# Gathers of a feed-forward layer's results add into X in place, two batches by turns

## The reference, cut to what matters

```python
x = x + tanh(g_xattn[0]) * L0_xattn(layernorm(x), ctx, ...)      # 16 heads
x = x + tanh(g_ffn[0])   * L0_ffn(layernorm(x), ...)             # 32 experts, top 4, and a shared one
x = x + tanh(g_xattn[1]) * L1_xattn(layernorm(x), ctx, ctx)      # 8 heads
x = x + tanh(g_ffn[1])   * L1_ffn(layernorm(x), ...)             # 8 experts, top 2, and shared ones

# the end of L0_ffn: each token sums four rows of the experts' results
gathered = ye[e_flat, minimum(pos, CAP - 1)]
gathered = where(valid, gathered, 0.0) * topk_w
routed   = gathered.reshape(T, K, D).sum(axis=1)
return routed + relu2(h @ shared_up_w.T) @ shared_down_w.T
```

## Time and profile before

| | us |
|---|---|
| median of 3 runs | 777.53 (777.05 to 778.8) |
| the profiled execution's own time | 779.62 |
| its span | 777.4 |
| busy PE, DVE, ACT, POOL | 667.8, 531.6, 379.0, 324.1 |
| the 64 gathers on POOL (L268) | 68.9, from 375.2 to 504.7 |
| mean granted TensorE clock | 0.955 of full speed |

### The profile page before, as it was taken

How to read it: one execution, slowest core, us unless ns; L and a number is a source line. 1 busy time by engine, 2 the same in 40 slices (tenths; PEclk the granted TensorE clock), 3 DMA queues, 4 the chain that set the end, 5 groups by cost and what they waited for, 6 DMA issues and landing times.

```text
span 777.4 us, 13620 instructions
## 1 busy us (share of the span) xinstructions
PE 667.8 (86%) x4737; PEld 349.5 (45%) x4738; DVE 531.6 (68%) x1252; ACT 379.0 (49%) x630; POOL 324.1 (42%) x337
## 2 busy tenths in 40 slices
PE   3889999999999899688735788999977999888996
PEld 1233333333333367576402244444433476555763
DVE  3889888888895699155278899997736743222336
ACT  2057888878787344244314566676502213333320
POOL 3535353535011101753568878831100057666530
PEclk9999999999999999889956999999979999999999
DMA  6834343444311800446447778896530022222137
GB/s 164 176 92 122 97 113 96 135 140 130 106 33 38 265 13 2 121 138 184 125 116 190 185 185 205 209 217 158 140 110 28 1 57 83 72 75 66 56 97 258
DMA packets 106362, 93.23 MB, mean 120 GB/s; under 512 B 25205, under 2 KB 92954, under 8 KB 106104
## 3 DMA queue, kind: packets, MB, share of 16 engines
q1 hardware_dynamic: 93600, 67.67, 32.5%
q0 software_dynamic: 8352, 18.74, 8.9%
q10 hardware_dynamic: 4344, 5.97, 2.9%
HBM read 50.63 MB, written 16.01 MB: 86 GB/s over the span
## 4 chain that ended last, share of the span: by engine, by line
PE 56%; DVE 13%; issue 11%; POOL 9%; DMA 4%; ACT 2%; SPq 2%; another core or an unknown queue 1%; ACTq 0%; POOLq 0%; DVEq 0%
PE O L447 9%; PE S L404 9%; PE ST L1547 6%; POOL spare L268 6%; DVE mx L566 4%; PE ST L1473 2%; PE S L1564 2%; PE M L1564 2%; PE ST L943 2%; POOL QKc L279 2%; PE ST L412 2%; PE M L496 2%; DMA QS<-mxT 2%; SPq L165 2%; PE M L489 1%
## 5 line engine op out<-in xcount | busy, mean ns | idle before, releaser
L566 DVE TENSOR_REDUCE mx<-S 128x2 f32<-128x512 f32 x384 | 250.7, 684 | 35.8 <-PE S L404 33.9
L319 ACT ACTIVATE PX<-ST 128x1024 f32<-128x1024 f32 x192 | 195.8, 1022 | 88.2 <-PE ST L412 79.2
L404 PE MATMUL S<-QS 62*128 62x256 bf16 (+1 forms) x768 | 151.2, 292 | 41.6 <-DVE mx L566 28.4
L412 PE MATMUL ST<-QS 64*128 64x256 bf16 (+1 forms) x768 | 141.0, 278 | 7.3 <-DMA QS<-mxT 7.3
L447 PE MATMUL O<-PX,VA 128*32 128x256 f32 x1536 | 123.3, 394 | 0.1
L404 PEld LDWEIGHTS S<-QS 62*128 62x128 bf16 (+1 forms) x768 | 48.7, 97 | 158.2 <-DVE mx L566 95.7
L268 POOL DMA_INDIRECT spare<-ye,GI x64 | 68.9, 1077 | 30.4 <-DMA ye<-QKc 16.1
L1658 POOL DMA_INDIRECT PX<-xn,TI x39 | 39.9, 1022 | 63.4 <-DVE K1n L1847 39.7
L412 PEld LDWEIGHTS ST<-QS 64*128 64x128 bf16 (+1 forms) x768 | 53.4, 96 | 23.3 <-DMA QS<-mxT 9.8
L1547 PE MATMUL ST<-EGU,Cb 128*128 x156 | 54.2, 471 | 6.3 <-ACT Cb L1615 4.9
L786 POOL DMA_INDIRECT PX<-xn,TI x32 | 33.5, 1046 | 61.2 <-DVE spare L1183 44.1
(11 more groups left out here) (302 smaller groups left out, 1114.2 us busy)
## 6 DMA issues: line engine op xcount, KB each, us to landing
QS<-QKs SPq DMA_DIRECT2D x177, 128.0 KB
EGU<-in_ew SPq DMA_DIRECT2D x16, 256.0 KB, 2.8
xn<-spare SPq DMA_DIRECT2D x8, 512.0 KB, 5.7
ye<-QKc SPq DMA_DIRECT2D x32, 128.0 KB
VA<-in_val SPq DMA_DIRECT2D x16, 256.0 KB
spare<-yt SPq DMA_DIRECT2D x16, 256.0 KB, 6.3
Cb<-in_ctx SPq DMA_DIRECT2D x31, 128.0 KB
on<-OS SPq DMA_DIRECT2D x27, 128.0 KB
```

The lines of the kernel that those rows point to most:

```text
L319: e.activation(M["PX"][pair % 4][:, :], M["ST"][pair % 2][:, :], ACT.Exp, scale=A.scale).then_inc(A.exp, 1)
L404: got = e.matmul(M["S"][n % 2][:, 256 * a:256 * a + 256], QS[:, 0, 128 * a:128 * a + 128], QS[:, 1, :], start=True, stop=True)
L412: got = e.matmul(M["ST"][(NP * t + k // 2) % 2][:, 512 * u + 256 * a:512 * u + 256 * a + 256], QS[:, 1, 128 * a:128 * a + 128], QS[:, 0, : ...
L566: e.tensor_reduce(M["mx"][b % 2][:, :, A.row_of_max(head)], M["S"][n % 2][:, :].rearrange("p (a s) -> p a s", a=2), AX.X, ALU.max, negate= ...
```

## The change

From batch 2 on, a gather no longer writes a buffer: it adds its rows into X[b] in place, through the transfer's own adding (`compute_op=ALU.add`). Two such gathers of one batch must not be under way together, since each reads X and writes it back. So a gather waits until the previous one of its batch has landed, and the order of the gathers takes two batches by turns: (2,0), (3,0), (2,1), (3,1), and so on, as batch and choice. It also waits for the shared expert's addition of its group. The bounds check of the indirect transfer is not given for these gathers. VectorE sums only batches 0 and 1; for the others `statistics` waits for the four gathers. The counts by the ends of steps -4, -3 and -2 become 12, 18 and 20.

```diff
--- before.py
+++ after.py
@@ -106,6 +106,8 @@
 
         self.s0 = 0 if self.first else 2
 
+        self.summed = 2
+
         self.lead = H + 12 if self.first else H + 6
 
     def steps(self):
@@ -116,7 +118,7 @@
 
     def gathered(self, t):
 
-        return {-5: 8, -4: 10, -3: 14, -2: 18, -1: 24, 0: 30, 1: 36}.get(t, max(0, min(K0 * (t + (7 if t < 0 else 8)), K0 * NB)))
+        return {-5: 8, -4: 12, -3: 18, -2: 20, -1: 24, 0: 30, 1: 36}.get(t, max(0, min(K0 * (t + (7 if t < 0 else 8)), K0 * NB)))
 
     def late(self, b):
 
@@ -235,7 +237,7 @@
             loads(e, w, t)
 
 
-def attention_pool(e, w, A, M, meanwhile=lambda t: None):
+def attention_pool(e, w, A, M, meanwhile=lambda t: None, shared=None):
     H = A.H
 
     for t in A.steps():
@@ -264,6 +266,17 @@
 
         def gather(n):
             b7, k = n // K0, n % K0
+            if b7 >= A.summed:
+
+                b7, k = b7 - b7 % 2 + k % 2, K0 // 2 * (b7 % 2) + k // 2
+                w.wait_ge(shared, b7 // GB + 1)
+
+                w.wait_ge(A.ga[b7 % 3], A.ga0 + 16 * (K0 * (b7 // 3) + k))
+                e.indirect_dma_start(
+                    out=M["X"][:, b7, :], out_offset=None, in_=M["ye_d"],
+                    in_offset=bass.IndirectOffsetOnAxis(ap=M["GI"][:, b7, k:k + 1], axis=0),
+                    compute_op=ALU.add).then_inc(A.ga[b7 % 3], 16)
+                return
             w.wait_ge(A.ca, 3 * (b7 - 2))
             e.indirect_dma_start(
                 out=M["GA"][b7 % 3][:, T * k:T * k + T], out_offset=None, in_=M["ye_d"],
@@ -547,8 +560,10 @@
         if b >= 2 * U:
 
             w.wait_ge(M["w_g"], 32)
-        if not A.first:
+        if not A.first and b < A.summed:
             w.wait_ge(A.ca, 3 * (b + 1))
+        elif not A.first:
+            w.wait_ge(A.ga[b % 3], A.ga0 + 16 * K0 * (b // 3 + 1))
         e.bn_stats(M["st6"][b % 2][:, :], M["X"][:, b, :]).then_inc(A.stat, 1)
         w.wait_ge(A.stat, 2 * b + 1)
         w.wait_ge(A.xn, b - 1)
@@ -656,12 +671,7 @@
                                     M["rs"][b0 % 2][:, 0:1], ALU.subtract, ALU.mult).then_inc(A.xn, 1)
                 if k in (3, 4) and within(b0) and b0 < A.helped:
                     parts(b0, k - 3)
-                if t == -2 and k == 4 or t == -1 and k == 0:
-                    for i in range(3):
-                        gathered(t + 4, i)
-                if t == -1 and 4 <= k < 7:
-                    gathered(b7, k - 4)
-                if t not in (-3, -2, -1) and 3 <= k < 6 and within(b7):
+                if 3 <= k < 6 and within(b7) and b7 < A.summed:
                     gathered(b7, k - 3)
                 if k == 6 and within(b6) and A.late(b6):
                     normalized(b6)
@@ -2248,7 +2258,7 @@
             w.wait_ge(X.dve, X.at["GI"])
             for k in range(4):
                 w.wait_ge(X.sty[k], 16 * E0 // 4)
-            attention_pool(e, w, L1, M, ffn1_pool_meanwhile(e, w, G1, M))
+            attention_pool(e, w, L1, M, ffn1_pool_meanwhile(e, w, G1, M), X.xa)
             ffn1_pool(e, w, G1, M)
 
         def act_program(e):
```

## The result

The changed kernel takes 802.88 us (median of 4 runs, 795.84 to 807.25) where the kernel before takes 777.29: 1.0312 times as long, 95% interval 1.0268 to 1.0356. I had forecast 773.8 us, and 790 as the upper end. It went the other way, by 25.6 us. The profiled execution took 802.34 us, with a span of 800.2.

A forecast was written before the change was run, and what follows sets the result against it. POOL was taken as first bound, VectorE second, with SP's queue also near full. Steps 0 to 8 gain 2.5 us and the ramp 1.2, so -3.7 from the 777.5 us median gives 773.8; range 768 to 790.

The forecast's parts named there:

- Two costs at nothing: POOL's time for an adding gather stays 1.05 us; steps behind the last gather count nothing, up to 1 us gained.
- rival 3: On POOL, building an adding gather costs 1.25 us for 1.05: +3.5 us, 781 us; chance 0.06.
- The landing L: Time until an adding gather has landed, which the next of its batch awaits: 4.0 us, from 3.43 plus 0.55.
- Rival 1: Waits of the turns bind POOL, with landings of 4.5 us or more: 784 at 4.5, 794 at 5; chance 0.22.
- The queue of the costs: Gather waits sit in POOL's program, delaying its subtractions and power, then ScalarE's second cut, SP's spreads and PE's scores.
- The walk through POOL's order: POOL's instructions added up in order, gathers waiting for landings: steps 0 to 8 take 83.1 us, 2.5 less.
- I count none of it directly: VectorE's removed sums, 26 us in all, lie beside POOL's chain and SP's transfers, so no direct gain was counted.
- SP's 8.4 us a step as the floor: SP's queue was held to need 8.4 us a step, stopping POOL from reaching its own 7.86 us.
- Moved: Earlier issue of gathers 10 to 19, in the ramp before batch 4's power: 1.2 us gained.
- Rival 2: The DMA engines become the bound in the gather steps, at 9.9 us a step: 786 us; chance 0.09.

The follow-up runs named there:

- the pair of two edits: Changed kernel with plain gathers into the old buffers, no turns, no sums for batches 2 to 15, and ScalarE issuing the row of maxima: 767.62 us, ratio 0.9867.

## Why the prediction was wrong, point by point

**The step that failed** is the first of "Two costs at nothing": "every indirect transfer in the trace takes about 1.0 us, so 1.05 stays". An adding gather takes POOL 1.56 us, 1.59 from start to start. I had this as rival 3, at 1.25 us and with a chance of 0.06. By the runs it is worth 17 to 18 of the 30 us lost, and it acts where POOL is the chain, as the earlier trace rows had said. The rows could show no such price: all of their gathers were plain writes, so all the trace said was that plain gathers agree with each other. The low chance treated that as evidence about an instruction of another kind. The bound above should have been the price of a second transfer's issue, another 1.0 us.

**The landing L** was mis-sized as well, at 4.0 us. The waits of the changed kernel give 4.0 to 4.4 us in the ramp and 4.6 to 6.1 later (5.2 in the mean of ten). With plain gathers by turns the same waits were 3.5 to 5.5 us, 4.7 in the mean of the seven in steps 0 to 8. So the part for the adding, 0.55 us in the prediction, was about right: it is some 0.5. What was too small is the landing of a plain gather, 3.43 us from three stalls of VectorE, all in the ramp. That the later steps' queues are fuller fits (DMA share 0.52 from 385 to 419 us and 0.81 from 450 to 505 in the kernel before), but it isn't the whole, as plain gathers by turns had 3.5 to 5.3 us in the ramp too. The data part of the transfer I had doubled from 0.55 to 1.1 us, and it became 0.92. Rival 1 had said 4.5 to 5, for 784 to 794; with plain gathers the turns gave 786, and in the changed kernel they cost 11.5 us.

**The queue of the costs was right.** The waits do sit in POOL's program, in front of the subtractions, and SP's spreads are what waits for them, 17.8 us. The walk through POOL's order gives the steps of the two adding kernels within a microsecond or so, once it has the measured sizes; without adding (76 us by the walk, 83.8 measured without sums) something else holds them.

**What VectorE is worth.** "I count none of it directly" held: some 2 to 4.5 us for 26 us of work. The reason that I gave, SP's 8.4 us a step as the floor, fell: with 1 us a step less on SP nothing moved, and in the run without sums SP waited 6.8 of 54 us, so by the prediction's own measure it needed 7.9 us a step and not 8.4, while the steps stayed at 9.0. The runs point to VectorE, POOL and the landing of the row of maxima standing at one height, which isn't shown; only the pair of two edits moved the steps, and what holds them at 8.5 us then stays open.

**Moved.** I had 1.2 us gained in the ramp, and with L = 4.0 a loss of 0.3. With plain gathers and the sums the new order shortens the ramp by 3.8 us in the profile; with adding and turns the ramp is 4.6 us longer. In time the order alone is 0.998 of before, and its interval (0.9947 to 1.0012) contains 1, so it can't be told from no effect.

**Rival 2** (DMA engines as the bound): the engines' time for a gather grew 1.7-fold, from 0.55 to 0.92 us, but the kernel with adding and no turns is explained by POOL's own time. No run here needs it. By the Trainium skill ("Collectives: The Full Stack", section "The bandwidth ceiling: the fold count and why AG ≠ RS ≠ AR") two source reads on one ring halve the rate of a collective that reduces. This case's queue came near that, with a factor of 1.7 in engine time; but its adding gathers also go in smaller packets, and no run parts the two.

**The range.** It ended at 790 because both sizes were bounded too low, and each alone would have passed it. By the prediction's own sums a landing of 5 us makes 794, which it left out, and 1.59 us a gather in place of 1.05 makes 98.0 us for steps 0 to 8 (12.3 more than before) and 8.6 more in the ramp, so 797. Together they cost less than their sum, since a gather that takes POOL longer hides more of the landing: for steps 0 to 8 the walk gives 83.1 us as forecast, 95.3 with a landing of 5, 98.0 with 1.59 us a gather, and 103.9 with both.

## What to carry to other kernels

When work is moved from one engine's arithmetic into a transfer, price the issue on the engine that builds the transfer, and don't take it from transfers of another kind; where the trace has none of the kind, double the nearest one for the upper end. An in-place sum turns independent transfers into a chain of landings: two by turns hide a landing only if the issuing engine has as much other work as the landing takes. And an engine that is 95% busy may still be worth almost nothing: ask first which second and third bound stands at its height.

## What the runs showed of the hardware

- An adding gather of 128 rows of 1 KB takes POOL 1.56 us, a plain one 1.03. The bounds check doesn't change it; with 64 rows it is 1.44.
- POOL's next instruction starts 1.0 us after an adding gather's start and overlaps it, but runs 0.55 to 0.6 us longer (1.75 for 1.17, 1.16 for 0.57). Pitches from start to start are to be read there, not durations.
- Its packets are smaller, 0.9 KB in the mean for 2.8: 3312 packets for 3.02 MB, where plain ones need 1275 for 3.51 MB. The 16 engines spend 0.92 us on it for 0.55.
- From its start to the start of the gather that waited for it pass 3.8 to 5.2 us, mostly near 4.1, when only one is under way; 4.0 to 6.1 us with two in the changed kernel, and up to 6.8 in the run with the bounds check.
- Chips differ: the kernel before took a median of 776.34 to 778.92 us in all comparisons but one, and 748.75 us in that one, on another chip. Only ratios of one chip are compared here.
